# Query features of the Fourier attention taken two units at a time, in a two-layer decoder kernel

## The chip, the cores and the metric

The kernel runs on one core of a Trainium2 chip. The metric is the device time of one execution in microseconds (us), lower is better; three runs of the kernel before gave 1551.49, 1552.3 and 1553.55, median 1552.3. Engines are named as in the profile: PE (matrix multiply), ACT (scalar), DVE (vector), POOL and SP.

## The reference, cut to what matters

Two decoder layers work on 64 sequences of 64 tokens of width 128. The change lies in one of the six sublayers, the self-attention of the second layer, which replaces softmax by random Fourier features. Cut to that:

```
def _fourier_kernel(x, proj_mat):
    p = jnp.einsum('blhd,dm->blhm', x, proj_mat) / math.sqrt(D_HEAD)
    return jnp.concatenate([jnp.cos(p), jnp.sin(p)], axis=-1) / math.sqrt(D_KMAP)
q = (x @ Wq.T + bq).reshape(Bv, Lv, N_HEAD, D_HEAD)      # 16 heads of 8
k = (x @ Wk.T + bk).reshape(Bv, Lv, N_HEAD, D_HEAD)
v = (x @ Wv.T + bv).reshape(Bv, Lv, N_HEAD, D_HEAD)
kv = jnp.einsum('blhm,blhd->bhmd', _fourier_kernel(k, proj_mat), v)
out = jnp.einsum('blhm,bhmd->blhd', _fourier_kernel(q, proj_mat), kv)
x = layernorm(x + out.reshape(Bv, Lv, D_MODEL) @ Wo.T + bo)
```

So every token and head gives 128 angles for the key and 128 for the query, each goes through a cosine and a sine, and two products use them: key features with values, then query features with that.

## The kernel before, in words

The program has three phases with a barrier between them. The second one, `experts_and_fourier_phase`, ends with the Fourier stage. It goes through G = 8 groups of T = 4 token tiles (512 tokens). A group has UPG = 16 units of 1024 angles per partition: units 0 to 7 are key units, units 8 to 15 query units (KEYS = 8). The running number of a unit is N; its number in the group is n. A unit passes these stations:

- PE, `angles` (L875): two matmuls write 1024 angles, in turns, into two banks of PSUM. There are two such pairs of banks, so the angles of unit N+2 wait until unit N is reduced (L887).
- DVE, `reduce_` (L1264): takes the whole turns off. In ten of the 16 units by two instructions (L1273, L1277); in the units of ON_SCALAR = 2, 5, 7, 10, 12, 14 ACT does the rounding (`lift`, L1091) and DVE needs one (L1270). Then the absolute value, `wrap` (L1281).
- ACT, `features` (L1063): a sine of `frac` (L1081) and, for the cosine, a sine of `wrap` with a bias of half a turn (L1085). `frac` and `wrap` have FRACS = 4 buffers.
- PE: for a key unit `key_values` (L899); for two query units together `outputs` (L950), which reads the features of four heads.

Between these stand the smaller works of a group. The key products are copied out by ACT (`keep_kv`, L1105), transposed by PE (`turn_key_values`, L947) and copied again (`keep_turned`, L1123). `outputs(g, q)`, q = 0 to 3, are copied out by `keep_o` (L1111), and after the fourth PE runs `combine` (L965, L974), the output projection of the group, in the middle of the next group. DVE then adds it to the stream (`residual`, L1288). The next group's inputs are transposed (`columns_of`, PE L859, ACT L1061), projected to keys and values (`keys_and_values`, L866, L868), and to queries (`queries`, L873).

The order on each engine is written out by hand: each engine runs its own loop over N, and each engine works strictly in its order. PE computes the angles of unit N+2 first in step N, then what belongs to the step. ACT lifts unit N+2 between the sine and the cosine of unit N. Nothing on ACT or PE is reordered at run time, so an instruction that waits holds all behind it.

Of the kernel before, what the change touches and what calls it, by code (L numbers as in the profile page):

```python
# [17 lines left out]
I32 = mybir.dt.int32  # L18
ALU = mybir.AluOpType
# [10 lines left out]
G = NT // T  # L30
# [679 lines left out]
def experts_and_fourier_phase(nc, ctx, c, name):  # L710
# [81 lines left out]
    with nc.Block() as block:  # L792
# [8 lines left out]
        def _(pe):  # L801
# [148 lines left out]
            def outputs(g, q):  # L950
                pe.wait_ge(s["feats"], g * UPG + KEYS + 2 * q + 2)
                if q == 0:
                    pe.wait_ge(s["kvT_sb"], 2 * g + 2)
                if q >= 2:
                    pe.wait_ge(s["o_sb"], g * Q4 + q - 1)
                for pair in range(T // 2):
                    toks = slice(pair * 2 * P, (pair + 1) * 2 * P)
                    for e in range(2):
                        for r in range(4):
                            last = nc.tensor.matmul(ps[32 * r:32 * r + 32, 4 + q % 2, toks],  # L960
                                                    kvm[:, pair, q, e, 32 * r:32 * r + 32], qf[:, q % 2, r, e, toks],
                                                    start=(e == 0), stop=(e == 1))
                last.then_inc(s["o_ps"], 1)
# [37 lines left out]
            for N in range(ALL + 5):  # L1001
                g, n = divmod(N, UPG)
                if N + 2 < ALL:
                    angles(N + 2)
                if g < G:
                    if 1 <= n <= KEYS:
                        key_values(N - 1)
                    if 3 <= N <= 6:
                        latent_products(N - 3)
                    if n == (8 if g == 0 else 6):  # L1010
                        turn_key_values(g, 0)
                    if n == 9:
                        turn_key_values(g, 1)
                    if n >= KEYS + 2 and n % 2 == 0:
                        outputs(g, n // 2 - 5)
                    if g + 1 < G:
                        if n == 10:
                            columns_of(g + 1)
                        if n == 11:
                            keys_and_values(g + 1)  # L1020
                        if n == 14:
                            queries(g + 1)
                if g >= 1:
                    if n == 0:
                        outputs(g - 1, Q4 - 1)
                    if n == 2:
                        combine(g - 1)

        @block.scalar
        def _(act):  # L1030
# [4 lines left out]
            def e_columns_of(g):  # L1035
                act.wait_ge(e["xT_ps"], g + 1)
                if g >= 2:
                    act.wait_ge(e["up"], (g - 1) * PARTS)
                    act.wait_ge(e["logits_ps"], g - 1)
                nc.scalar.copy(e_xT[:, g % 2, :], ps[:, XT, :]).then_inc(e["xT_sb"], 1)  # L1040
# [18 lines left out]
            def columns_of(g):  # L1059
                act.wait_ge(s["xT_ps"], g + 1)  # L1060
                nc.scalar.copy(xT[:, :], ps[:, x_bank(g), :]).then_inc(s["xT_sb"], 1)  # L1061

            def features(N):  # L1063
                g, n = divmod(N, UPG)
                act.wait_ge(s["reduced"], N + 1)
                if n < KEYS:
                    used = g * KEYS + n - RING + 1 if n >= RING else g * KEYS
                    if used >= 1:
                        act.wait_ge(s["kv_ps"], used)
                    sin, cos = feats[:, n % RING, :, 1, :], feats[:, n % RING, :, 0, :]  # L1070
                    view = lambda a: a.rearrange("p (h m) -> p h m", m=M)
                else:
                    v = n - KEYS
                    if v % 2 == 0:
                        used = g * Q4 + v // 2 - 1
                        if used >= 1:
                            act.wait_ge(s["o_ps"], used)
                    h = (v % 2) * 2
                    sin, cos = qf[:, (v // 2) % 2, h:h + 2, 1, :], qf[:, (v // 2) % 2, h:h + 2, 0, :]
                    view = lambda a: a.rearrange("p (h m) -> p h m", h=2)  # L1080
                nc.scalar.activation(sin, view(frac[:, N % FRACS, :]), ACT.Sin, scale=-TWO_PI)  # L1081
                if N + 2 < ALL and (n + 2) % UPG in ON_SCALAR:
                    lift(N + 2)
                act.wait_ge(s["wrapped"], N + 1)
                nc.scalar.activation(cos, view(wrap[:, N % FRACS, :]), ACT.Sin, bias=half_pi[:, :], scale=-TWO_PI).then_inc(s["feats"], 1)  # L1085

            def lift(N):
                act.wait_ge(s["z_ps"], N + 1)
# [32 lines left out]
            def keep_turned(g, pair):  # L1121
                act.wait_ge(s["kvT_ps"], 2 * g + pair + 1)
                nc.scalar.copy(kvm[:, pair, :, :, :], ps[:, 6:8, :].rearrange("p a (b e m) -> p (a b) e m", b=2, e=2)).then_inc(s["kvT_sb"], 1)  # L1123

            e_columns_of(0)
            root(1, LATE)
            exponent(0)
# [13 lines left out]
            for N in range(ALL + 5):  # L1141
                g, n = divmod(N, UPG)
                if g < G:
                    if N == KEYS:
                        act.wait_ge(s["ab_ps"], 4)
                        act.wait_ge(e["lowered"], PIECES)
                        act.wait_ge(e["measured"], 2 * G)
                    if N == KEYS - 2:
                        root(3, LATE)
                    features(N)  # L1150
                    if 3 <= N <= 6:
                        keep_products(N - 3)
                    if g >= 1 and n == 2:
                        queries(g)
                    if n == 4:
                        keep_kv(g, 0)
                    if g == 0 and n == 8:
                        keep_turned(g, 0)
                    if n == 8:
                        keep_kv(g, 1)  # L1160
                    if g >= 1 and n == 7:
                        keep_turned(g, 0)
                    if n == 9:
                        keep_turned(g, 1)
                    if n >= KEYS + 3 and n % 2 == 1:
                        keep_o(g, (n - KEYS - 3) // 2)
                    if n == 10 and g + 1 < G:
                        columns_of(g + 1)
                    if n == 12 and g + 1 < G:
                        keys(g + 1)  # L1170
                if g == G and n == 0:
                    act.wait_ge(s["var"], 1)
                    nc.scalar.activation(c["rstd"][:, 0:MEASURED], c["rstd"][:, 0:MEASURED], ACT.Sqrt)
                    nc.scalar.activation(rstdc[:, :], rstdc[:, :], ACT.Sqrt).then_inc(s["root"], 1)
                if g >= 1:
                    if n == 1:
                        keep_o(g - 1, Q4 - 1)
                if g == G and n == 2:
                    act.wait_ge(s["var2"], 1)
                    nc.scalar.activation(rstd2[:, 0:MEASURED], rstd2[:, 0:MEASURED], ACT.Sqrt).then_inc(s["root2"], 1)  # L1180

        @block.vector
        def _(dve):
# [80 lines left out]
            def reduce_(N):  # L1264
                n = N % UPG
                z = angles_at(N)
                part = frac[:, N % FRACS, :]
                if n in ON_SCALAR:
                    dve.wait_ge(s["lifted"], lifts_before(N) + 1)
                    nc.vector.scalar_tensor_tensor(part, part, MAGIC, z, ALU.subtract, ALU.subtract).then_inc(s["reduced"], 1)  # L1270
                else:
                    dve.wait_ge(s["z_ps"], N + 1)
                    nc.vector.tensor_scalar(whole[:, :], z, MAGIC, MAGIC, ALU.add, ALU.subtract).then_inc(s["rounded"], 1)  # L1273
                    dve.wait_ge(s["rounded"], N - lifts_before(N) + 1)
                    if N >= FRACS:
                        dve.wait_ge(s["feats"], N - FRACS + 1)
                    nc.vector.tensor_tensor(part, whole[:, :], z, ALU.subtract).then_inc(s["reduced"], 1)  # L1277
                dve.wait_ge(s["reduced"], N + 1)
                if N >= FRACS:
                    dve.wait_ge(s["feats"], N - FRACS + 1)  # L1280
                nc.vector.tensor_scalar(wrap[:, N % FRACS, :].bitcast(I32), part.bitcast(I32), 0x7FFFFFFF, None,  # L1281
                                        ALU.bitwise_and).then_inc(s["wrapped"], 1)

            def residual(g):
                x = c["stream"][:, g * T:(g + 1) * T, :]
# [1244 lines left out]
```

## Time and profile before

| | before |
|---|---|
| median of three runs | 1552.3 us |
| the profiled execution itself | 1550.78 us |
| its span in the profile | 1549.0 us |
| mean granted clock of PE | 0.977 |
| busy over the span | PE 91%, DVE 72%, ACT 63% |
| Fourier stage, first sine to last (L1081) | 506.2 to 890.5 us |

The span is the stretch from the first to the last instruction of one execution; the time of that execution has 1.8 us more around it. A row of the timeline gives start, duration, engine, line, operation and tiles. The duration of an ACT or DVE instruction overlaps the start of the next by about a tenth, so for a row of instructions the distance from start to start is what each costs; the end counts for whoever waits for the result. Rows of PE join consecutive matmuls of one line; a matmul of 32-bit numbers is recorded as more than one.

### The profile page before, as it was taken

To read this page: it belongs to the slowest core of one execution; us is meant where nothing else is said; L and a number is where in the kernel's file an instruction comes from. 1 tells how busy PE (TensorE), PEld (TensorE's weight loads), DVE (VectorE), ACT (ScalarE), POOL (GpSimd) and SP (SyncE) were. 2 spreads that over 40 slices of the span, in tenths; PEclk is the share of its full clock that TensorE was granted. 3 is DMA by queue.
4 is the path that set the end of the run, shared out by engine and by line. 5 is a ranking of instruction groups with operands and counts; after the bars stand their busy time and mean duration, and the time that the engine had idled before them with its cause. 6 is when DMAs were issued, how large, how long until landed. Compare 5 with 4: busy or idle time off the path is not lost. (4 is left out here: it accounts for less than half of the span.)

```text
span 1549.0 us, 32429 instructions
## 1 busy us (share of the span) xinstructions
PE 1410.6 (91%) x12666; PEld 864.9 (56%) x12666; DVE 1112.9 (72%) x2348; ACT 979.0 (63%) x1524; POOL 297.6 (19%) x274
## 2 busy tenths in 40 slices
PE   6999999998899799898998878999999999999984
PEld 4666666666566344343443354666666666666652
DVE  4666778886433899999999954355667776776688
ACT  2233367676555899999999954455555665665546
POOL 3433244452001011110110031111111221220000
PEclk9999999999899999999999999999999999999996
DMA  5000000000100000000000002222222222222210
GB/s 185 3 2 2 2 15 16 13 9 3 55 1 1 1 2 1 1 1 1 1 1 4 1 14 59 70 64 64 64 62 62 62 62 62 62 62 62 69 42 21
DMA packets 40246, 49.74 MB, mean 32 GB/s; under 512 B 8992, under 2 KB 22944, under 8 KB 39712
## 3 DMA queue, kind: packets, MB, share of 16 engines
q1 hardware_dynamic: 39808, 47.01, 11.8%
q8 instruction: 102, 1.67, 0.5%
q10 hardware_dynamic: 288, 0.67, 0.2%
q14 instruction: 48, 0.39, 0.1%
HBM read 13.04 MB, written 2.10 MB: 10 GB/s over the span
## 5 line engine op out<-in xcount | busy, mean ns | idle before, releaser
L2065 DVE TENSOR_TENSOR l_px<-psum,l_share 128x1024 f32<-128x1024 f32 x64 | 78.4, 1225 | 152.3 <-PE psum L1572 102.1
L1810 ACT ACTIVATE l_prob<-psum,l_bias 128x1024 f32<-128x1024 f32 x64 | 71.4, 1115 | 174.1 <-PE psum L1543 174.1
L1555 PE MATMUL psum<-l_XT,l_A 128*128 128x256 f32 x512 | 125.3, 389 | 1.1 <-ACT l_XT L1828 1.1
L1538 PE MATMUL psum<-l_th,l_XT 128*128 128x512 f32 x256 | 124.1, 607 | 1.6 <-DVE stream L2072 0.8
L1572 PE MATMUL psum<-l_prob,l_X 128*128 128x512 f32 x256 | 121.3, 596 | 0.7 <-DVE l_px L2065 0.7
L1618 PE MATMUL psum<-l_px,l_N 128*128 128x256 f32 x480 | 115.0, 383 | 0.0
L2042 DVE TENSOR_REDUCE l_top<-psum 128x8 bf16<-128x1024 f32 x64 | 78.2, 1221 | 36.6 <-PE psum L1635 36.6
L1555 PEld LDWEIGHTS psum<-l_XT,l_A 128*128 128x128 f32 x512 | 93.5, 192 | 11.9 <-ACT l_XT L1828 1.4
L1277 DVE TENSOR_TENSOR f_frac<-f_whole,psum 128x1024 f32<-128x1024 f32 x80 | 97.7, 1221 | 2.7
L1273 DVE TENSOR_SCALAR f_whole<-psum 128x1024 f32<-128x1024 f32 x80 | 97.4, 1218 | 1.6 <-PE psum L894 1.6
L1618 PEld LDWEIGHTS psum<-l_px,l_N 128*128 128x128 f32 x480 | 87.6, 190 | 16.1 <-issue 5.0
L408 ACT ACTIVATE a_probT<-psum 128x1024 f32<-128x1024 f32 x32 | 32.8, 1025 | 98.5 <-PE psum L199 98.5
L1815 ACT COPY l_th<-psum 128x1024 f32<-128x1024 f32 x64 | 64.8, 1012 | 45.5 <-PE psum L1555 45.5
L1281 DVE TENSOR_SCALAR f_wrap<-f_frac 128x1024 int32<-128x1024 int32 x128 | 88.8, 694 | 4.4
L894 PE MATMUL psum<-f_projX,f_kT 64*128 64x512 f32 x256 | 74.0, 654 | 11.5 <-DVE f_frac L1277 8.0
L915 PE MATMUL psum<-f_feats,f_vS 128*32 128x256 f32 x1024 | 69.4, 389 | 15.5 <-ACT f_feats L1085 8.3
L669 POOL TENSOR_TENSOR a_KX<-a_KT,const 128x1024 f32<-128x1024 f32 x32 | 60.8, 1904 | 113.2 <-ACT a_KT L375 89.1
L480 DVE TENSOR_TENSOR a_prob<-psum,relbias 128x1024 f32<-128x1024 f32 x32 | 39.2, 1225 | 56.5 <-PE psum L185 51.0
L399 ACT ACTIVATE c_QX<-c_QT,const 128x128 f32<-128x128 f32 x256 | 78.7, 404 | 0.0
L2365 POOL TENSOR_TENSOR l_hn<-l_hh,late_weights 128x1024 f32<-128x1024 f32 x12 | 28.2, 2349 | 247.4 <-DVE l_hh L2123 247.4
L960 PE MATMUL psum<-f_qf,f_kvm 128*32 128x256 f32 x1024 | 63.4, 389 | 12.9 <-ACT f_kvm L1123 6.7
L1401 POOL TENSOR_SCALAR f_xs<-stream,moments,rstd 128x128 f32<-128x128 f32 x28 | 24.5, 885 | 263.2 <-PE psum L859 263.0
(355 smaller groups left out, 3243.8 us busy)
## 6 DMA issues: line engine op xcount, KB each, us to landing
l_share<-l_recip SPq DMA_DIRECT2D x496, 64.0 KB, 2.0
early_weights<-in_weights SPq DMA_DIRECT2D x1, 2405.0 KB, 11.2
c_cs<-in_ctx SPq DMA_DIRECT2D x16, 128.0 KB, 2.1
f_qf<-in_l_mats SPq DMA_DIRECT2D x1, 2048.0 KB, 7.8
out<-l_normed SPq DMA_DIRECT2D x16, 128.0 KB, 2.0
l_craw<-in_ctx SPq DMA_DIRECT2D x15, 128.0 KB, 2.3
late_weights<-in_weights SPq DMA_DIRECT2D x1, 1089.0 KB, 11.2
relbias<-in_relbias ACTq DMA_DIRECT2D x1, 512.0 KB, 5.1
```

What stands on the lines that cost most here:

```text
L399: last = nc.scalar.activation(QX[:, n % 3, :, j, :], QT[:, d % DUOS, t * P:(t + 1) * P].rearrange("p (b s) -> p b s", s=S), ACT.Copy, scal ...
L894: last = nc.tensor.matmul(out, kT[rows, t * P:(t + 1) * P], projX[rows, h:h + 4, :], start=True, stop=True)
L1273: nc.vector.tensor_scalar(whole[:, :], z, MAGIC, MAGIC, ALU.add, ALU.subtract).then_inc(s["rounded"], 1)
L1277: nc.vector.tensor_tensor(part, whole[:, :], z, ALU.subtract).then_inc(s["reduced"], 1)
L1281: nc.vector.tensor_scalar(wrap[:, N % FRACS, :].bitcast(I32), part.bitcast(I32), 0x7FFFFFFF, None, ALU.bitwise_and).then_inc(s["wrapped"], 1)
L1538: nc.tensor.matmul(ps[:, SC + n, :], XT[:, q % 3, k, :, :], th[:, q % 2, k, 8 * n:8 * n + 8, :], start=True, stop=False)
L1555: last = nc.tensor.matmul(ps[:, at + j // 2, (j % 2) * 256:(j % 2 + 1) * 256], A[:, QB * k + j, :], XT[:, q % 3, :, 1, :], start=True, sto ...
L1572: last = nc.tensor.matmul(ps[:, at + n, :], X[:, q % 2, k, :], prob[:, b % 4, n, :], start=True, stop=True)
L1618: last = nc.tensor.matmul(ps[:, YB, 0:256], N[:, h, :], px[:, q % 2, h, :, :], start=(h == 0), stop=(h == H - 1))
L1810: nc.scalar.activation(prob[:, b % 4, :, :], ps[:, SC:SC + 2, :], ACT.Exp, bias=bias[:, b:b + 1]).then_inc(s["exped"], 1)
L2042: nc.vector.tensor_reduce(top[:, b % 4, :], ps[:, RO:RO + 2, :].rearrange("p a (j n) -> p (a j) n", n=P), AX.X, ALU.max, negate=True).then ...
L2065: nc.vector.tensor_tensor(px[:, q % 2, :, k, :], ps[:, at:at + 2, :].rearrange("p a (h s) -> p (a h) s", s=S), share[:, (b // 2) % 2, b % ...
```

## The change

On ACT, the two query units of a pair are taken by one sine and one cosine over 2048 columns, in steps n = 9, 11, 13 and 15, by a new function `query_features`. In step 8 ACT now does the lift of unit 10 alone, with no feature instruction. Lifts of units 12 and 14 follow the cosine of the pair two before. The copies `keep_turned(g, 1)` and `columns_of(g + 1)` stand between the sine and the cosine of the first and the second pair. On DVE one `wrap` covers both units of a pair. On PE each `outputs` moves to the next step: those of a group to n = 11, 13 and 15, and the fourth to n = 1 of the next group, where it stands behind `key_values` of unit 0.

```diff
                         turn_key_values(g, 1)
-                    if n >= KEYS + 2 and n % 2 == 0:
-                        outputs(g, n // 2 - 5)
+                    if n >= KEYS + 3 and n % 2 == 1:
+                        outputs(g, (n - KEYS - 3) // 2)
...
                 if g >= 1:
-                    if n == 0:
+                    if n == 1:
                         outputs(g - 1, Q4 - 1)
...
+            def query_features(N, between):
+                g, n = divmod(N, UPG)
+                v = n - KEYS
+                at = N % FRACS
+                act.wait_ge(s["reduced"], N + 2)
+                used = g * Q4 + v // 2 - 1
+                if used >= 1:
+                    act.wait_ge(s["o_ps"], used)
+                sin, cos = qf[:, (v // 2) % 2, :, 1, :], qf[:, (v // 2) % 2, :, 0, :]
+                view = lambda a: a[:, at:at + 2, :].rearrange("p n (h m) -> p (n h) m", h=2)
+                nc.scalar.activation(sin, view(frac), ACT.Sin, scale=-TWO_PI)
+                between(g)
+                act.wait_ge(s["wrapped"], N + 2)
+                nc.scalar.activation(cos, view(wrap), ACT.Sin, bias=half_pi[:, :], scale=-TWO_PI).then_inc(s["feats"], 2)
+                if n + 4 in ON_SCALAR:
+                    lift(N + 4)
...
-                    features(N)
+                    if n < KEYS:
+                        features(N)
+                    elif n % 2 == 1:
+                        query_features(N - 1, {9: second_turned, 11: next_columns}.get(n, lambda g: None))
+                    elif n + 2 in ON_SCALAR and n == KEYS:
+                        lift(N + 2)
...
-                    if n == 9:
-                        keep_turned(g, 1)
...
-                    if n == 10 and g + 1 < G:
-                        columns_of(g + 1)
...
+                units = 2 if n >= KEYS else 1
                 dve.wait_ge(s["reduced"], N + 1)
+                if units == 2 and n % 2 == 0:
+                    return
+                at = (N + 1 - units) % FRACS
                 if N >= FRACS:
                     dve.wait_ge(s["feats"], N - FRACS + 1)
-                nc.vector.tensor_scalar(wrap[:, N % FRACS, :].bitcast(I32), part.bitcast(I32), 0x7FFFFFFF, None,
-                                        ALU.bitwise_and).then_inc(s["wrapped"], 1)
+                nc.vector.tensor_scalar(wrap[:, at:at + units, :].bitcast(I32), frac[:, at:at + units, :].bitcast(I32), 0x7FFFFFFF, None,
+                                        ALU.bitwise_and).then_inc(s["wrapped"], units)
```

PE at the border of two groups, before, from the projection of the next queries (L873) on. L896 and L894 are angles (of query and of key units), L960 is `outputs`, L915 `key_values`, L974 `combine`:

```order
L873 MATMUL psum<-f_xT,early_weights 128x512
L894 MATMUL psum<-f_projX,f_kT 128x512 x4
L960 MATMUL psum<-f_qf,f_kvm 32x256 x16
L894 MATMUL psum<-f_projX,f_kT 128x512 x2
L915 MATMUL psum<-f_feats,f_vS 32x256 x8
L894 MATMUL psum<-f_projX,f_kT 128x512 x2
L915 MATMUL psum<-f_feats,f_vS 32x256 x8
L974 MATMUL psum<-early_weights,f_oT 64x128 x32
L894 MATMUL psum<-f_projX,f_kT 128x512 x2
```

The same place in the changed kernel:

```order
L873 MATMUL psum<-f_xT,early_weights 128x512
L894 MATMUL psum<-f_projX,f_kT 128x512 x2
L960 MATMUL psum<-f_qf,f_kvm 32x256 x16
L894 MATMUL psum<-f_projX,f_kT 128x512 x4
L915 MATMUL psum<-f_feats,f_vS 32x256 x8
L960 MATMUL psum<-f_qf,f_kvm 32x256 x16
L894 MATMUL psum<-f_projX,f_kT 128x512 x2
L915 MATMUL psum<-f_feats,f_vS 32x256 x8
L974 MATMUL psum<-early_weights,f_oT 64x128 x32
L894 MATMUL psum<-f_projX,f_kT 128x512 x2
```

The fourth `outputs` of a group stood ahead of the first L915 of the next group; now it stands behind it. The third, which stood ahead of L873 (and so outside the first piece), now stands behind it.

ACT from the copy of the first transposed key products (`keep_turned`) to the lift of unit 12, before:

```order
L1123 COPY f_kvm<-psum 128x1024
L1081 ACTIVATE f_qf<-f_frac 128x2x512
L1091 ACTIVATE f_frac<-psum 128x1024
L1085 ACTIVATE f_qf<-f_wrap,f_half_pi 128x2x512
L1105 COPY f_kvs<-psum 128x1024
L1081 ACTIVATE f_qf<-f_frac 128x2x512
L1085 ACTIVATE f_qf<-f_wrap,f_half_pi 128x2x512
L1123 COPY f_kvm<-psum 128x1024
L1081 ACTIVATE f_qf<-f_frac 128x2x512
L1091 ACTIVATE f_frac<-psum 128x1024
```

In the changed kernel, from the same copy to the lift of unit 14 (L1131 is now `keep_turned`, L1099 `lift`, L1113 `keep_kv`, L1088 the pair's sine, L1091 the pair's cosine):

```order
L1131 COPY f_kvm<-psum 128x1024
L1099 ACTIVATE f_frac<-psum 128x1024
L1113 COPY f_kvs<-psum 128x1024
L1088 ACTIVATE f_qf<-f_frac 128x4x512
L1131 COPY f_kvm<-psum 128x1024
L1091 ACTIVATE f_qf<-f_wrap,f_half_pi 128x4x512
L1099 ACTIVATE f_frac<-psum 128x1024
L1088 ACTIVATE f_qf<-f_frac 128x4x512
L1061 COPY f_xT<-psum 128x512
L1091 ACTIVATE f_qf<-f_wrap,f_half_pi 128x4x512
L1099 ACTIVATE f_frac<-psum 128x1024
```

The lift of unit 10 moved ahead of all query features; each later lift now stands behind a cosine of 2048 columns; the copy of `f_xT`, which the next group's projections on PE wait for, stands behind the second pair's sine.

## Rows read from the trace of the kernel before

**Rows 1.** The page: ACT in 40 slices, tenths busy.

```profile
ACT  2233367676555899999999954455555665665546
```

**Rows 2.** One period of the stage, busy time of each engine.

```profile
667.95:715.60 47.65, 42.46 (x420) 19.41 (x422) 45.15 (x56) 44.75 (x50) 5.28 (x5) 1.00 0.00 1
```

**Rows 3.** Timeline of ACT: the lift of unit 5 in groups 1, 4 and 7.

```profile
572.67 1.02 ACT L1091 ACTIVATE f_frac<-psum 128x1024 f32<-128x1024 f32 x1 [2.84 <-PE psum L894]
...
715.60 1.02 ACT L1091 ACTIVATE f_frac<-psum 128x1024 f32<-128x1024 f32 x1 [2.85 <-PE psum L894]
...
858.54 1.02 ACT L1091 ACTIVATE f_frac<-psum 128x1024 f32<-128x1024 f32 x1 [2.84 <-PE psum L894]
```

**Rows 4.** Timeline of DVE: the same wait in each group, unit 12.

```profile
689.28 1.22 DVE L1270 SCALAR_TENSOR_TENSOR f_frac<-f_frac,psum 128x1024 f32<-128x1024 f32 x1 [1.32 <-ACT f_frac L1091]
690.54 0.69 DVE L1281 TENSOR_SCALAR f_wrap<-f_frac 128x1024 int32<-128x1024 int32 x1
```

**Rows 5.** Timeline of ACT, group 3: lift of unit 5, then a stretch without waits.

```profile
667.95 1.02 ACT L1091 ACTIVATE f_frac<-psum 128x1024 f32<-128x1024 f32 x1 [2.84 <-PE psum L894]
...
671.90 1.00 ACT L1105 COPY f_kvs<-psum 128x1024 f32<-128x1024 f32 x1
672.79 1.07 ACT L1081 ACTIVATE f_feats<-f_frac 128x1024 f32<-128x1024 f32 x1
673.75 1.02 ACT L1091 ACTIVATE f_frac<-psum 128x1024 f32<-128x1024 f32 x1
674.66 1.15 ACT L1085 ACTIVATE f_feats<-f_wrap,f_half_pi 128x1024 f32<-128x1024 f32 x1
675.70 1.06 ACT L1081 ACTIVATE f_feats<-f_frac 128x1024 f32<-128x1024 f32 x1
...
688.21 1.04 ACT L1091 ACTIVATE f_frac<-psum 128x1024 f32<-128x1024 f32 x1
...
690.16 0.61 ACT L1061 COPY f_xT<-psum 128x512 f32<-128x512 f32 x1
690.62 1.10 ACT L1081 ACTIVATE f_qf<-f_frac 128x1024 f32<-128x1024 f32 x1
...
696.12 0.68 ACT L1099 ACTIVATE f_kT<-psum,f_kb 128x512 f32<-128x512 f32 x1
696.69 1.05 ACT L1081 ACTIVATE f_qf<-f_frac 128x1024 f32<-128x1024 f32 x1
```

**Rows 6.** Timeline of PE, group 3 and the border to group 4.

```profile
675.86 1.07 PE L915 MATMUL psum<-f_feats,f_vS 128*32 128x256 f32 x16 [0.66 <-ACT f_feats L1085]
...
681.00 1.07 PE L915 MATMUL psum<-f_feats,f_vS 128*32 128x256 f32 x16
...
691.03 1.12 PE L866 MATMUL psum<-f_xT,early_weights 128*128 128x512 f32 x2
...
692.98 1.13 PE L896 MATMUL psum<-f_qT,f_projX 64*128 64x512 f32 x4
694.04 1.93 PE L960 MATMUL psum<-f_qf,f_kvm 128*32 128x256 f32 x32
...
708.72 1.13 PE L894 MATMUL psum<-f_projX,f_kT 64*128 64x512 f32 x4
709.78 1.07 PE L915 MATMUL psum<-f_feats,f_vS 128*32 128x256 f32 x16
710.78 3.71 PE L974 MATMUL psum<-early_weights,f_oT 128*64 128x128 f32 x64
714.42 1.13 PE L894 MATMUL psum<-f_projX,f_kT 64*128 64x512 f32 x4
```

**Rows 7.** Group 0, ACT: sine of unit 8; PE: the first transposes.

```profile
536.75 1.05 ACT L1081 ACTIVATE f_qf<-f_frac 128x1024 f32<-128x1024 f32 x1
...
537.90 1.09 PE L947 MATMUL psum<-const,f_kvs 128*128 128x128 f32 x8
```

**Rows 8.** Group 7, ACT: the copy of the third `outputs`, last before the roots.

```profile
892.54 0.62 ACT L1111 COPY f_oT<-psum 128x512 f32<-128x512 f32 x1
```

More of the change, by code:

```diff
@@ L1071, in features @@
                     view = lambda a: a.rearrange("p (h m) -> p h m", m=M)
[L1072 to L1080, printed above, removed]
                 nc.scalar.activation(sin, view(frac[:, N % FRACS, :]), ACT.Sin, scale=-TWO_PI)
@@ L1123, in keep_turned, with second_turned, next_columns @@
                 nc.scalar.copy(kvm[:, pair, :, :, :], ps[:, 6:8, :].rearrange("p a (b e m) -> p (a b) e m", b=2, e=2)).then_inc(s["kvT_sb"], 1)
+            def second_turned(g):
+                keep_turned(g, 1)
+            def next_columns(g):
+                if g + 1 < G:
+                    columns_of(g + 1)
             e_columns_of(0)
```

## Prediction

> **What bounds the kernel now.** The page's slices come first: ACT is at nine tenths or more only from the fifteenth to the twenty-second of 40 slices [rows 1], and that is the Fourier stage, the only place the change touches. The timeline then shows that the stage is periodic. The lift of unit 5 starts at 572.67 in group 1 and at 858.54 in group 7 [rows 3], six periods of 47.65 us. Within one period [rows 2] ACT is busy 44.75, DVE 45.15, PE 42.46 us at a granted clock of 1.00. No engine is full, so the sum of no one engine's work gives the period. What gives it is a chain that closes on itself, and I look for it by the two waits that recur: ACT waits 2.84 us for PE's angles ahead of the lift of unit 5 [rows 3], and DVE waits 1.32 us for ACT's lift of unit 12 [rows 4].
>
> From these the chain reads: ACT works without a wait from the lift of unit 5 to that of unit 12, 667.95 to 688.21, 20.26 us [rows 5]. DVE takes that lift 1.07 later, at 689.28 [rows 4]. DVE then works on to unit 2 of the next group, for which PE's angles of unit 4 start at 708.72, 19.44 later. PE does angles, `key_values`, `combine` and the angles of unit 5, to 715.55 [rows 6], and ACT lifts at 715.60: 6.88. Together 47.65. Each hand-over costs about 0.05, as between the cosine's end at 674.66 + 1.15 and PE at 675.86 [rows 5, 6].
>
> **Prices.** Start to start on ACT [rows 5]: copy of 1024 columns 0.89, of 512 columns 0.46, so 0.43 for 512 and 0.86 for 1024 more columns; sine 0.96; lift 0.91; cosine 1.04 (1.15 to its end); `f_kT` 0.57. No row shows a sine over 2048 columns. I take a second thousand at the slope: sine 0.96 + 0.86 = 1.82, cosine 1.90, and 2.01 to its end. The bounds: nothing but the slope (1.72 for either) below, twice the single price (1.92 and 2.08) above. On PE [rows 6]: `key_values` 1.00, angles 1.06 (1.13 to the end), `combine` 3.64, the two projections 1.95 (691.03 to 692.98), `outputs` 1.93 less the 0.06 that neighbours overlap, 1.87.
>
> **What the change saves.** On ACT a pair costs 0.10 + 0.18 less, four pairs 1.1 us in a group. On DVE four instructions of `wrap` go. One takes 0.69 [rows 4] against 1.22 of the other instructions of equal width; I take the pair's at the rate of the single one, below 1.38, some 0.1 saved a pair. Neither engine's total sets the period, so this is worth only what falls on a closed chain.
>
> **What it moves, and the new chain.** The old chain gets shorter: the sine of unit 10 leaves it (0.96), one pair is merged (0.28), and since the lift of unit 12 must see the end of the cosine just ahead of it, 2.01 + 0.05 instead of 1.90, 0.16 comes back; DVE's part loses 0.2. That alone would be 46.4. But three moves make another chain. The fourth `outputs` now stands on PE behind `key_values` of unit 0, which waits for ACT's cosine of unit 0; behind both stand the angles of unit 4, `combine` and the angles of unit 5. Before, `outputs` ran while ACT was still at unit 0, beside other work; now its 1.87 is between ACT and ACT. The lift of unit 10 moved ahead of the features into a place where PE isn't ready. And the copy of `f_xT`, now behind the second pair's sine, releases PE's projections, behind which stand the angles of unit 14, for which ACT's next lift waits. I lay this out from 667.95:
>
> 1. As before to the end of the cosine of unit 5: 7.86, at 675.81 [rows 5].
> 2. PE as before from 675.86 to the end of `key_values` of unit 7, 681.00 + 1.07: 6.26, at 682.07 [rows 6]. ACT is there early: from 674.66 it has 1.04, two sines and two cosines, and the copy, 5.93, to 680.59. It waits for the angles of unit 10 (ends about 681.07, lift to 682.03), then for these key products.
> 3. ACT: 0.05, copy 0.89, sine 1.82, copy 0.89, cosine 2.01, 0.05, lift 0.91, sine 1.82, `f_xT` to its end 0.61: 9.05, at 691.12. DVE has the lift of unit 12 at 688.8, so it isn't late.
> 4. PE: 0.05, projections 1.95, angles of unit 14 1.13: 3.13, at 694.25. ACT has waited about 1.2 for this.
> 5. ACT: 0.05, lift 0.91, copy 0.46, `f_kT` 0.57, sine 1.82, cosine 1.90, copy 0.46, sine 1.82, cosine 1.90, copy 0.46, sine 0.96, lift 0.91, cosine of unit 0 to its end 1.15: 13.37, at 707.62.
> 6. PE: 0.05, `key_values` 1.00, `outputs` 1.87, angles 1.06, `key_values` 1.00, `combine` 3.64, angles of unit 5 1.13, and 0.05 to the lift: 9.80, at 717.42.
>
> The period is 49.47 against 47.65, 1.8 more; six periods 10.9. DVE, started at 688.8 with 19.4 less 0.2 to go, could release unit 4's angles at 708.1, and PE gets to them at 710.5: DVE no longer bounds, and it will wait for `combine` at the residual.
>
> **Head and tail.** In group 0 ACT reaches the lift of unit 10 at 536.75, and its next copy needs PE's transposes, done at 537.90 + 1.09 [rows 7]. With 0.05 and 0.89 the copy of the key products starts at 539.93. Steps 3 to 6 without the first 0.05 make 35.30, so the lift of unit 5 in group 1 comes at 575.23, against 572.67: 2.6 later. In group 7 there are no next inputs. From the lift of unit 5 to the last copy before the roots it was 892.54 - 858.54 = 34.00 [rows 3, 8]. Now it is 14.17 to the copy of the key products, then 0.89 + 1.82 + 0.89 + 2.06 + 0.91 + 1.82 + 2.06 + 0.91 + 0.46 + 1.82 + 1.90 + 0.46 + 1.82 + 1.90 = 19.72, so 33.89: 0.1 less. The third phase starts behind a barrier and is only shifted.
>
> The sum is 2.6 + 10.9 - 0.1 = 13.4; with rows rounded to 0.01 over some 30 terms I take 13. Against the profiled execution, 1550.8, that gives 1564; it lay 1.5 below the median of the runs, 1552.3, so against the median it is 1565.
>
> **A page that speaks against this.** ACT is busy 44.75 of 47.65 us and DVE 45.15 [rows 2], 94 and 95%. The Trainium skill, Perfetto Trace Analysis, Optimizing Scalar/DVE Operations, says that grouping into larger operations can raise throughput if the engine is saturated, and, two paragraphs on, that where these engines aren't saturated but cause bubbles elsewhere, splitting may finish work sooner. By the first sentence this change gains what rival A below gains; by the second, which the 2.84 us wait of ACT bears out, it loses.
>
> **Rivals.**
>
> A, faster. The new chain doesn't close, and the old one, shortened to 46.4, sets the period: 1.2 in 6.5 periods, 8 us, 1544. For it speaks that both engines are over 90% busy and both get less work. Against it, DVE's release is 2.4 us ahead of PE at the angles of unit 4. It decides if step 6 is free of `outputs`, that is, if the period of steps 1 to 6 falls below 46.4. Chance 5%.
>
> B, no change. The chain is there, but shorter by the whole 1.8, since wide activations cost less than the slope says and hand-overs overlap; time 1552. With the lower bounds (four sines and three cosines of pairs in the chain, 0.10 and 0.18 each) it loses 0.9, which isn't enough alone. Chance 5%.
>
> C, far slower. `wrap` over two buffers loses its rate and costs 1.22 per 1024 columns, 1.1 more a pair, 4.3 a group. DVE then has 45.15 + 4.3 and waits of its own, 50 to 52 a period: 20 to 30 us, 1572 to 1582. The view is one contiguous run, as before, which speaks against it. Chance 4%.
>
> **Numbers.** The forecast has 86%. Its own bounds: the lower price of wide activations takes 0.9 a period off, 6 us (1559); the upper adds as much (1571). The range I give is 1557 to 1572, which leaves room for a part of B below. About 0.2% (3 us) is what a measurement of this kernel can tell from no change. Faster by more 0.05, within it 0.06, slower 0.89.
>
> **What would show it.** Right: the lift of unit 5 returns every 49.2 to 49.7 us; ACT has waits at the lift of unit 10 (0.5), the lift of unit 14 (over 1) and at the lift of unit 5 (about 2.8); on PE the fourth `outputs` follows `key_values` of unit 0 with no gap, and PE waits for `f_xT`; DVE waits for `combine` at L1308, the residual, which was free before. The pair's sine takes about 1.9, its cosine 2.0. Wrong: a period below 48.5, DVE without that wait, or a pair's `wrap` above 1.4.

## The result: slower, by more than was forecast

| | before | changed |
|---|---|---|
| median of the runs | 1552.3 us | 1575.47 us (1574.21 to 1576.47) |
| profiled execution, its span | 1550.78, 1549.0 | 1574.89, 1573.1 |
| period of the Fourier stage | 47.65 | 51.14 |
| mean granted clock of PE, whole span | 0.977 | 0.971 |

The ratio is 1.015, with an interval of 1.0135 to 1.0165: 23 us where 13 were forecast, outside the range of 1557 to 1572. The page of the changed kernel shows it in its slices: ACT, which stood at nine tenths through the stage [rows 1], now stands at eight in all but one of them, and neither PE nor DVE has taken its place.

```profile
PE   6999999997999888898888878999999999999984
...
DVE  4666778886435788988898863455667677776788
ACT  2333367766555888988888854345556655666546
```

ACT's timeline in the changed kernel gives the period (L1099 is the lift). The lift of unit 5 stands at 574.46 in group 1 and 881.25 in group 7, 306.79 for six periods, against 285.87 in [rows 3]:

```profile
574.46 1.02 ACT L1099 ACTIVATE f_frac<-psum 128x1024 f32<-128x1024 f32 x1 [2.65 <-PE psum L894]
...
676.67 1.02 ACT L1099 ACTIVATE f_frac<-psum 128x1024 f32<-128x1024 f32 x1 [2.65 <-PE psum L894]
...
727.81 1.02 ACT L1099 ACTIVATE f_frac<-psum 128x1024 f32<-128x1024 f32 x1 [2.65 <-PE psum L894]
...
881.25 1.02 ACT L1099 ACTIVATE f_frac<-psum 128x1024 f32<-128x1024 f32 x1 [2.65 <-PE psum L894]
```

The rest of ACT's group 3, from the end of the key part on, answers to [rows 5] and has the waits and prices that were forecast: 0.45 ahead of the lift of unit 10, 1.27 ahead of that of unit 14, a pair's sine 1.81 start to start, its cosine 1.89 to 1.90 (2.01 to its end):

```profile
689.83 1.02 ACT L1099 ACTIVATE f_frac<-psum 128x1024 f32<-128x1024 f32 x1 [0.45 <-PE psum L896]
690.85 1.01 ACT L1113 COPY f_kvs<-psum 128x1024 f32<-128x1024 f32 x1
691.76 1.92 ACT L1088 ACTIVATE f_qf<-f_frac 128x2048 f32<-128x2048 f32 x1
693.57 1.00 ACT L1131 COPY f_kvm<-psum 128x1024 f32<-128x1024 f32 x1
694.46 2.01 ACT L1091 ACTIVATE f_qf<-f_wrap,f_half_pi 128x2048 f32<-128x2048 f32 x1
696.57 1.03 ACT L1099 ACTIVATE f_frac<-psum 128x1024 f32<-128x1024 f32 x1
...
699.29 0.58 ACT L1061 COPY f_xT<-psum 128x512 f32<-128x512 f32 x1
...
703.04 1.02 ACT L1099 ACTIVATE f_frac<-psum 128x1024 f32<-128x1024 f32 x1 [1.27 <-PE psum L896]
...
715.20 1.18 ACT L1076 ACTIVATE f_feats<-f_wrap,f_half_pi 128x1024 f32<-128x1024 f32 x1
```

PE at the border of groups 3 and 4, against the last four rows of [rows 6]. Read the start to start distances: `key_values` (L915) takes 1.60, `outputs` (L960) 2.81, where 1.00 and 1.87 were taken; ahead of them stand three waits of PE.

```profile
711.84 1.13 PE L894 MATMUL psum<-f_projX,f_kT 64*128 64x512 f32 x4 [0.72 <-DVE f_frac L1293]
714.95 1.13 PE L894 MATMUL psum<-f_projX,f_kT 64*128 64x512 f32 x4 [1.98 <-DVE f_frac L1293]
716.52 1.90 PE L915 MATMUL psum<-f_feats,f_vS 128*32 128x256 f32 x16 [0.44 <-ACT f_feats L1076]
718.12 2.88 PE L960 MATMUL psum<-f_qf,f_kvm 128*32 128x256 f32 x32
720.93 1.13 PE L894 MATMUL psum<-f_projX,f_kT 64*128 64x512 f32 x4
```

The same stretch in windows of 2 us of the changed kernel. The columns are the window and its length, then busy time and number of instructions of PE, of its weight loads, of DVE, ACT and POOL, then the granted clock as a share of 2.4 GHz. PE is all but idle from 713 to 715; the clock is 0.90 in the next window, 0.50, which is 1.2 GHz, from 717 to 719, and back at 1.00 from 721 on:

```profile
713.00:715.00 2.00, 0.05 (x2) 0.05 (x2) 1.93 (x3) 2.00 (x3) 0.00 (x0) 1.00 0.00 0
715.00:717.00 2.00, 1.56 (x12) 0.61 (x16) 1.97 (x3) 2.00 (x3) 0.00 (x0) 0.90 0.00 0
717.00:719.00 2.00, 2.00 (x25) 1.23 (x21) 1.97 (x3) 1.36 (x2) 0.00 (x0) 0.50 0.03 8
719.00:721.00 2.00, 2.00 (x30) 1.16 (x22) 1.57 (x2) 0.00 (x0) 0.00 (x0) 0.74 0.00 0
721.00:723.00 2.00, 2.00 (x22) 0.66 (x22) 0.89 (x1) 1.94 (x3) 0.00 (x0) 1.00 0.00 0
```

DVE's timeline of the changed kernel: the residual waits for `combine`, as forecast, and a pair's `wrap` takes 1.23, 1.14 start to start, so it keeps its rate.

```profile
675.61 0.69 DVE L1308 TENSOR_TENSOR stream<-psum,stream 128x512 f32<-128x512 f32 x1 [1.44 <-PE psum L974]
...
690.46 1.23 DVE L1301 TENSOR_SCALAR f_wrap<-f_frac 128x2048 int32<-128x2048 int32 x1
691.60 1.22 DVE L1286 SCALAR_TENSOR_TENSOR f_frac<-f_frac,psum 128x1024 f32<-128x1024 f32 x1
```

Where the 24.1 us between the two spans are, before against changed: the first sine comes at 506.17 and at 504.25, 1.9 less; from it to the lift of unit 5 in group 1, 66.50 and 70.21, 3.7 more; six periods, 20.9 more; from there to the last copy ahead of the roots, 34.00 and 33.96, nothing; from that copy to the end of the span, 656.5 and 657.9, 1.4 more. The code of the first and the last of these stretches is the same in both kernels; their differences, of opposite sign, are left unexplained.

### The profile page after: what moved, and what is told of

It is laid out like the page before. It is cut to its first block and busy times, and to the rows that moved or that the text cites. A ratio compares the mean times of both kernels' runs of the same rounds, so it can differ in the third digit from the quotient of the medians.

```text
span 1573.1 us, 32364 instructions
## 1 busy us (share of the span) xinstructions
PE 1422.2 (90%) x12666; PEld 872.0 (55%) x12666; DVE 1112.1 (71%) x2316; ACT 972.0 (62%) x1460; POOL 297.7 (19%) x274
## 5 line engine op out<-in xcount | busy, mean ns | idle before, releaser
L894 PE MATMUL psum<-f_projX,f_kT 64*128 64x512 f32 x256 | 72.8, 645 | 24.0 <-DVE f_frac L1293 24.0
L915 PE MATMUL psum<-f_feats,f_vS 128*32 128x256 f32 x1024 | 75.8, 418 | 18.7 <-ACT f_feats L1076 11.6
L408 ACT ACTIVATE a_probT<-psum 128x1024 f32<-128x1024 f32 x32 | 32.8, 1024 | 96.4 <-PE psum L199 96.4
L1301 DVE TENSOR_SCALAR f_wrap<-f_frac 128x1024 int32<-128x1024 int32 (+1 forms) x96 | 83.7, 872 | 5.1
L915 PEld LDWEIGHTS psum<-f_feats,f_vS 128*32 128x32 f32 x1024 | 29.1, 115 | 83.0 <-issue 29.6
```

The source lines that it names most:

```text
L915: last = nc.tensor.matmul(ps[32 * r:32 * r + 32, 4 + q // 2, (q % 2) * 256:(q % 2 + 1) * 256], vS[:, t % 2, t // 2, head_of(place), :], fe ...
L1301: nc.vector.tensor_scalar(wrap[:, at:at + units, :].bitcast(I32), frac[:, at:at + units, :].bitcast(I32), 0x7FFFFFFF, None, ALU.bitwise_an ...
```

## The experiments

The theory after the result, K: the period has two additions. The fourth `outputs` on the chain and the late hand-overs make 1.8 us, as forecast; another 1.6 are PE's clock, which falls behind the idle stretch that the same move opens. The rival W: the new order costs 3.5 by itself, in the instructions or in waits, whatever the clock. All periods below are read as above, over four to six groups.

| kernel | period | median | ratio to before (interval) |
|---|---|---|---|
| changed | 51.14 | 1575.5 | 1.015 (1.0135 to 1.0165) |
| changed, PE's gap filled | 49.46 | 1566.6 | 1.0088 (1.0072 to 1.0104) |
| changed, fourth outputs back | 48.05 | 1552.4 | 1.0001 (0.9987 to 1.0015) |
| changed, all outputs back | 51.25 | 1575.8 | 1.016 (1.0134 to 1.0187) |
| before, fourth outputs late | 51.0 | 1574.5 | 1.0143 (1.0127 to 1.0159) |
| the same, PE's gap filled | 49.36 | 1563.4 | 1.0071 (1.0048 to 1.0093) |
| changed, fourth back, f_xT early | 47.23 | 1549.2 | 0.9982 (0.9967 to 0.9997) |
| the same, lift of unit 5 later | 46.48 | 1542.6 | 0.9933 (0.9913 to 0.9953) |
| before, lift of unit 5 later | 46.77 | 1545.5 | 0.9953 (0.9935 to 0.997) |

**Fill the gap.**

```diff
+            def filler(g):
+                pe.wait_ge(s["v_sb"], g + 1)
+                nc.tensor.matmul(ps[:, 6, :], w("f_wq"), kT[:, :], start=True, stop=True)
+                nc.tensor.matmul(ps[:, 6, 0:256], w("f_wq"), kT[:, 0:256], start=True, stop=True)
...
+                if 1 <= g < G and n == 0:
+                    filler(g)
```

> The changed kernel with one and a half extra matmuls of 512 columns on PE (about 1.6 us of work into a free PSUM bank, their result never read) in step 0 of each group, where PE sat idle 1.98 us ahead of the angles of unit 3. Nothing is taken from the chain through the fourth outputs. Theory K (the 1.6 us of a period that the forecast lacked are PE's granted clock, which fell to 1.2 GHz behind that idle stretch): key_values of unit 0 takes 1.0 and the fourth outputs 1.9 again, the period falls from 51.1 to 49.4 to 49.6, the time from 1575 to about 1565. Rival W (the extra time belongs to the order itself, key_values and outputs being slow there for what they read, or a wait for ACT): the period stays at 51.1 and the time at 1575 or a little more.

PE's timeline of this kernel at the same border, and one window over it. L967 and L968 are the extra matmuls. The angles of unit 3 (at 712.17) still wait for the same DVE instruction, but the wait is 0.50; start to start, `key_values` takes 0.86 and `outputs` 1.86.

```profile
710.11 1.13 PE L967 MATMUL psum<-f_kT,early_weights 128*128 128x512 f32 x2
711.07 0.59 PE L968 MATMUL psum<-f_kT,early_weights 128*128 128x256 f32 x2
712.17 1.13 PE L894 MATMUL psum<-f_projX,f_kT 64*128 64x512 f32 x4 [0.50 <-DVE f_frac L1300]
713.73 1.07 PE L915 MATMUL psum<-f_feats,f_vS 128*32 128x256 f32 x16 [0.43 <-ACT f_feats L1083]
714.59 1.94 PE L960 MATMUL psum<-f_qf,f_kvm 128*32 128x256 f32 x32
716.45 1.13 PE L894 MATMUL psum<-f_projX,f_kT 64*128 64x512 f32 x4
...
710.00:716.00 6.00, 5.07 (x54) 2.69 (x56) 5.86 (x7) 5.56 (x7) 0.00 (x0) 1.00 0.01 3
```

The granted clock is 1.00 in the window from 710 to 716 and in the next one. More work on PE made the kernel 9 us faster. K stands, W doesn't: at an unchanged order nothing but the filling and the clock differs, and 1.68 us of the period go. They are the 0.74 that `key_values` takes less and the 0.95 that `outputs` takes less. The hand-over is not part of them: ACT's cosine of unit 0 starts at 712.41 here and takes 1.17, and PE starts 0.15 later, as in the changed kernel. The period, 49.46, is within 0.01 of the 49.47 of the prediction's steps; so close a match has some luck in it, since in step 6 the hand-over is 0.10 longer than was taken and `key_values` 0.14 shorter.

**The fourth outputs back in step 0**, everything else as changed.

```diff
-                    if n == 1:
+                    if n == 0:
                         outputs(g - 1, Q4 - 1)
```

> The changed kernel with the fourth outputs of a group back in step 0, ahead of key_values of unit 0; everything else as changed. Theory: its 1.87 leave the chain between ACT's cosine of unit 0 and ACT's lift of unit 5, and it fills PE's idle stretch, so the clock stays at 2.4 GHz: period 47.8 to 48.1, time 1553 to 1557, within 0.3% of before. Rival (pairing on ACT is what costs: late copies and lifts): the period stays above 49 and the time above 1562.

The loss is gone whole; the period is at the upper end of what the theory gave, the time, 1552.4, just below it. PE's timeline shows how the place fits: the pair's cosine is done just ahead, `outputs` takes what was the idle stretch, and the angles of unit 3 follow without a wait.

```profile
701.63 1.13 PE L894 MATMUL psum<-f_projX,f_kT 64*128 64x512 f32 x4 [0.71 <-DVE f_frac L1293]
702.83 1.93 PE L960 MATMUL psum<-f_qf,f_kvm 128*32 128x256 f32 x32
704.75 1.13 PE L894 MATMUL psum<-f_projX,f_kT 64*128 64x512 f32 x4
706.31 1.07 PE L915 MATMUL psum<-f_feats,f_vS 128*32 128x256 f32 x16 [0.43 <-ACT f_feats L1076]
```

One digit in the code was worth 23 us. The pairs save ACT its 1.1 us a group and yet the period is 0.4 longer than before: the saving is not on the chain that binds here.

**The same move in the kernel before**, the only edit, features single.

```diff
-                    if n == 0:
+                    if n == 1:
                         outputs(g - 1, Q4 - 1)
```

> The kernel before with one edit: the fourth outputs of a group from step 0 to step 1, behind key_values of unit 0. Features stay single. Theory (this one move makes the loss): DVE's release of unit 4's angles now meets a PE that has 1.87 more to do first, the period goes to 49.5; PE idles some 2 us ahead of the angles of unit 3, so the clock falls as in the changed kernel and adds 1 to 1.6: period 50.5 to 51.2, time 1570 to 1577. Rival (the loss needs the pairs): period 47.6 to 48, time about 1553.

The move alone makes the loss. PE's timeline at the border: the idle stretch is there too (1.99), and behind it the angles take 1.42 start to start instead of 1.06, `key_values` 1.71, `outputs` 2.29; together 1.5 more than at the full clock.

```profile
716.50 1.49 PE L894 MATMUL psum<-f_projX,f_kT 64*128 64x512 f32 x4 [1.99 <-DVE f_frac L1277]
717.92 1.94 PE L915 MATMUL psum<-f_feats,f_vS 128*32 128x256 f32 x16
719.63 2.37 PE L960 MATMUL psum<-f_qf,f_kvm 128*32 128x256 f32 x32
721.92 1.13 PE L894 MATMUL psum<-f_projX,f_kT 64*128 64x512 f32 x4
```

**And with the gap filled there too**: the edit just shown and the filler of the first experiment.

> The kernel before with the fourth outputs in step 1 (alone it had a period of 51.0), and 1.6 us of extra matmuls on PE in step 0, their result never read. Theory K (two parts: 1.9 us on the chain, 1.5 us from the clock): the clock is 1.00 through the group border, the period 49.4 to 49.6, the time 1564 to 1567. Rival (in this kernel DVE, not ACT, releases PE there, and extra work on PE comes on top): period 51 or more, time 1575 or more.

The period falls from 51.0 to 49.36 and the clock is 1.00 from 600 to 880; period and time (1563.4) come out just below what K gave, and far from the rival. So each of the two parts is seen in both kernels: 1.6 to 1.7 from the clock, 1.7 to 1.8 from the chain.

**All four outputs back**, only the pairs on ACT and DVE kept.

```diff
-                    if n >= KEYS + 3 and n % 2 == 1:
-                        outputs(g, (n - KEYS - 3) // 2)
+                    if n >= KEYS + 2 and n % 2 == 0:
+                        outputs(g, n // 2 - 5)
...
-                    if n == 1:
+                    if n == 0:
                         outputs(g - 1, Q4 - 1)
```

> The changed kernel with all four outputs in their old steps on PE, only the pairs on ACT and DVE kept. Theory: PE now waits for the whole pair's cosine ahead of angles that DVE needs, so ACT and PE hand over more often: period 48.2 to 48.5, time 1557 to 1560, slower than before by 0.3 to 0.5%. Rival (pairs save 1.1 us of ACT a group, which shows once PE's order is the old one): period below 47.3, time below 1550.

Both expectations missed: 51.25, as slow as the changed kernel. PE now waits 2.46 us for the first pair's cosine and the `outputs` behind it takes 3.15 instead of 1.87; the third, behind a wait of 1.73 ahead of angles, takes 3.55. The granted clock is 0.93 from 600 to 700, with 0.57 from 696 to 700.

```profile
695.72 3.22 PE L960 MATMUL psum<-f_qf,f_kvm 128*32 128x256 f32 x32 [2.46 <-ACT f_qf L1091]
698.87 1.00 PE L859 MATMUL psum<-const,f_xs 128*128 128x128 f32 x4
...
708.59 1.13 PE L894 MATMUL psum<-f_projX,f_kT 64*128 64x512 f32 x4 [1.73 <-DVE f_frac L1286]
709.81 3.62 PE L960 MATMUL psum<-f_qf,f_kvm 128*32 128x256 f32 x32
713.36 1.12 PE L873 MATMUL psum<-f_xT,early_weights 128*128 128x512 f32 x2
```

I expected this kernel by the same arithmetic at the full clock that had failed once already. With pairs on ACT, the first three `outputs` are better one step later; only the fourth isn't. No run fills the gap in this kernel, so how much of its loss is the clock stays open; the two slow `outputs` alone took 2.96 longer than at the full clock, and the period is 3.6 longer than before.

**The copy of f_xT early.** With the fourth outputs back, the chain left is that of steps 3 and 4: ACT's sine, the copy, PE's projections, angles, ACT's lift of unit 14.

```diff
-                        query_features(N - 1, {9: second_turned, 11: next_columns}.get(n, lambda g: None))
+                        if n == 11:
+                            next_columns(g)
+                        query_features(N - 1, {9: second_turned}.get(n, lambda g: None))
```

> The changed kernel with the fourth outputs back in step 0 and ACT's copy of the next group's inputs ahead of the second pair's sine instead of behind it. Theory (the chain of steps 3 and 4, ACT sine, copy, projections, angles of unit 14, lift, is the one that now sets the period of 48.05): 1.8 us of PE's wait go, ACT's wait of 1.27 at the lift of unit 14 is gone, period 47.0 to 47.2, time 1546 to 1549. Rival (the chain over DVE's unit 12 to unit 2 sets it, as before the change): period 47.9 to 48.1, time as the kernel with the fourth outputs back, 1552.

The period is 47.23, 0.82 less than with the copy late: the theory's side, though just above its 47.0 to 47.2. ACT's wait of 1.27 at the lift of unit 14 is gone, and so is PE's wait for `f_xT`, which was 1.46 and not the 1.8 expected. The time, 1549.2, is at the upper end of what was expected. Against the kernel before it is 0.2% less, with an interval from 0.03% to 0.33%, so hardly clear of nothing.

**The lift of unit 5 behind the cosine of unit 3.** In every kernel so far ACT stands still for 2.35 to 2.85 us at that lift, with the cosine of unit 3 ready behind it. The edit in `features`, in the last kernel and alone in the kernel before:

```diff
-                if N + 2 < ALL and (n + 2) % UPG in ON_SCALAR:
+                if N + 2 < ALL and (n + 2) % UPG in ON_SCALAR and n != 3:
                     lift(N + 2)
...
+                if n == 3:
+                    lift(N + 2)
```

> As the kernel with the fourth outputs back and the early copy, and the lift of unit 5 moved behind the cosine of unit 3 on ACT, so that ACT does the cosine in place of a part of its 2.7 us wait for PE's angles of unit 5. Theory: ACT's path to the lift of unit 12 gets 1.04 shorter; period 46.2 to 46.5, time 1540 to 1544, 0.6% below the kernel before. Rival (DVE needs the lift of unit 5 at once and loses what ACT gains): period 47.0 or more, time 1547 or more.

> The kernel before with the lift of unit 5 behind the cosine of unit 3 as its only edit, features single. Theory (ACT's segment from the lift of unit 5 to that of unit 12 is part of the chain that sets the period, and gets 1.04 shorter, until another chain binds): period 46.7 to 46.9, time 1546 to 1549. Rival: no change, 47.65 and 1552 to 1553.

Both theories held, with the time of the second, 1545.5, just below its range. In the kernel with pairs the period is 46.48, the time 1542.6, which beats both kernels, by 0.67% the one before. ACT's timeline shows the cosine moved into the wait, which shrank by 1.03 (from 2.62 to 1.59):

```profile
664.43 1.06 ACT L1072 ACTIVATE f_feats<-f_frac 128x1024 f32<-128x1024 f32 x1
665.38 1.15 ACT L1076 ACTIVATE f_feats<-f_wrap,f_half_pi 128x1024 f32<-128x1024 f32 x1
668.11 1.02 ACT L1101 ACTIVATE f_frac<-psum 128x1024 f32<-128x1024 f32 x1 [1.59 <-PE psum L894]
```

Alone in the kernel before, the same edit gives 46.77 and 1545.5. The periods fell by 0.75 and by 0.88, not by the whole 1.04 that the cosine takes. In the kernel before, ACT's part from the lift of unit 5 to that of unit 12 went from 20.26 to 19.40 (664.99 to 684.39), for the copy of the key products now starts 0.17 later behind the cosine than it would back to back; the rest of the chain took 27.39 and takes 27.37. This is the plainest evidence that the chain which the prediction read is the one that sets the period. So of the gain most is this edit, and the pairs add at best 0.3 us a period; the intervals of the two ratios overlap (0.9913 to 0.9953, 0.9935 to 0.997), so that they add anything to the time isn't shown.

## Why the prediction was wrong, point by point

- That a chain through three engines sets the period, and which: right. Every period above moved by edits on it, not by the engines' sums. In the changed kernel PE, DVE and ACT all had less or equal work in a group and the period grew.
- Steps 1 to 5, forecast 7.86, 6.26, 9.05, 3.13, 13.37, measured in group 3: 7.85 (676.67 to 684.52), 6.26 (to 690.78), 9.09 (to 699.87), 3.12 (to 702.99, which is the lift at 703.04 less a hand-over of 0.05), 13.39 (to 716.38). Right within 0.04 each, and with them the price of a wide sine and cosine, the waits of 0.5 and 1.2, and DVE's rate.
- Step 6, forecast 9.80, measured 11.43 (716.38 to 727.81): this is the step that failed. `key_values` took 1.60 against 1.00, `outputs` 2.81 against 1.87, the hand-over 0.14 against 0.05, 1.63 together. The 6.88 that follow are as forecast. The durations of `key_values` and `outputs` had been taken from rows at 2.4 GHz, and the text held the granted clock at 1.00 without laying out what PE does ahead of the step. Had it done so, it would have found the gap: the move that puts `outputs` on the chain takes it out of the stretch ahead of the angles of unit 3. The run with the gap filled shows the clock as the cause of the two long durations, and not of the hand-over, which stays at 0.15 there.
- The trace before did show the price. In group 7, PE's timeline of the kernel before has an `outputs` behind 2.37 us of idle that takes 3.40 instead of 1.93, at a granted clock of 0.50 from 888.3 to 891.3:

```profile
888.28 3.40 PE L960 MATMUL psum<-f_qf,f_kvm 128*32 128x256 f32 x32 [2.37 <-ACT f_qf L1085]
```

- Six periods: 10.9 forecast, 20.9 measured, of which step 6 is 9.8. Head: 2.6 forecast, 3.7 measured; there too `key_values` and `outputs` of the border ran slow, 1.68 and 2.53 start to start. Tail: -0.1 forecast, 0.0 measured.
- One reading of the page of the profile was off by one: the slices with ACT at nine tenths run to the twenty-third, not the twenty-second. No term of the sum uses it.
- Rival A (the old chain, shortened, sets the period) is refuted for this change by the period of 51.14. The first sentence that was taken from the Trainium skill (Perfetto Trace Analysis, Optimizing Scalar/DVE Operations), larger operations where the engine is saturated, gave no gain at 94 and 95% busy: the run with the fourth outputs back has all its savings on ACT and is no faster, and with the copy early too the period is 0.42 below that of before. That sentence speaks of a saturated engine, and ACT, with its waits, was not one. The second sentence from the same section of the Trainium skill, on engines that cause bubbles elsewhere, is nearer to what the run with all outputs back shows: the wide cosine makes PE wait 2.46. Rival B (wide activations cheaper) and C (`wrap` loses its rate) are refuted by the durations. None of them named the clock. The range took in wrong prices of ACT's work and no wrong price of PE's.

## What to carry to other kernels

Lay the period out as a chain over the engines, and then lay out PE's idle stretches too, before and after the edit: work that was moved out of a gap onto the chain was paid here once for its length, 1.8 us a period, and once more for the clock of what ran behind the gap, 1.6. Before pricing a step on PE at the full clock, look in the trace for the same instruction behind a similar idle stretch. Where an in-order engine waits at an instruction and the one behind is ready, exchange the two before merging anything: that was worth 7 us here, and the merging on top of it perhaps 3, which the intervals don't tell from nothing.

## What the runs showed of the hardware

Extra matmuls whose result nobody reads made the kernel faster, by 9 and by 11 us in two kernels; with them the granted clock stayed at 1.00. Not every wait of PE is followed by a lower clock. In the kernel before, the longest waits in a middle group were 0.66 us at the border and 1.10 elsewhere, and the clock stayed at 1.00; in the changed kernel a wait of 1.45 for `f_xT` (ahead of 699.92) left it at 1.00 too. At the waits of 1.73 to 2.46 us in the middle groups of three kernels (changed, fourth `outputs` late, all `outputs` back) the clock went to 0.50 within 2 us, every time, and matmuls ran at or near half speed for some 3 us. But the length of the wait alone doesn't decide it: in group 7 of the kernel before, a wait of 2.37 ended with the clock at 0.50, and in group 7 of the same kernel with the lift of unit 5 later, waits of 2.37 and 2.52 (ahead of the `outputs` at 880.96 and 885.41) left it at 1.00. What decides is not shown by these runs.

A sine over 2048 columns took 1.92 us, one over 1024 took 1.05 to 1.11; start to start 1.81 and 0.95, so that the second thousand columns costs 0.86, as the copies of 512 and 1024 columns had let expect. An ACT instruction that waits for the end of the one just ahead on ACT starts 0.10 after it: the cosine at 694.46 + 2.01, the lift at 696.57.
